# Adjacency product of a GNN layer, rearranged: x stationary, adj streamed 512 nodes wide into two alternating PSUM banks

## The chip, the core and the metric

The program runs on one core of a Trainium2 chip. The metric is the device time of one execution in microseconds; the kernel before takes 399.12 us (median of 3 runs, 398.97 to 399.54). "PE" is TensorE, "DVE" VectorE, "ACT" ScalarE, "POOL" GpSimd, "SP" SyncE, from whose queue the DMAs are issued.

## The reference

```python
support = x @ weight                                 # x (4096, 256), weight (256, 256)
h = (1.0 - t) * support + t * (adj @ support)        # adj (4096, 4096), about 0.1% full, t a scalar (1.0 in the data)
out = layernorm(x + h)                               # over the 256 features, eps 1e-5, all float32
```

Since the products are linear, h is also ((1 - t) x + t (adj @ x)) @ weight. The kernel before forms the product with weight first, the changed one last.

## The kernel before

Every float32 operand is split into a high part, rounded to the PE's float32r format (`*_hi`, a Copy on ACT), and a low part, the difference (`*_lo`, a subtraction on DVE or POOL). A product of two such operands is three products: high by high, high by low, low by high. In a matmul on the PE one operand, 128x128, is loaded first and stays (the stationary one, a LDWEIGHTS in the trace), and the other streams past it, one column per step.

**S stage** (`s_round`, L319): S = x @ W for 32 tiles of 128 nodes. Transposed x arrives in 16 chunks of 256 KB (`load_x`, L116, four slots); ACT makes `x_hi` (L168), POOL `x_lo` (L215). For a tile, six matmuls of 256 columns (L331, L336, L341) add up in half of a PSUM bank `s_ps`; a bank holds two tiles, so twelve matmuls in a row write one bank. ACT (L173) writes the high part of S beside the low part (DVE, L247), so that S has 512 columns per block of 128 nodes, high then low.

**Adjacency stage** (`adj_round`, L345): for each of 32 tiles of 128 output nodes, and each of 32 blocks j of 128 input nodes, the stationary operand is a 128x128 block of transposed adj. `high()` (L361) streams the 512 columns of S[j] past the high part of the block; `low()` (L366) streams the 256 high columns of S[j] past its low part, into the right half of the same bank. A tile owns one bank (`agg[u]`, u the parity of the tile), so 64 matmuls in a row write one bank. adj comes in 64 chunks of 1 MB (`load_adj`, L120), four slots (two per tile); ACT makes `a_hi` (L180), DVE `a_lo` (L253), each in one instruction of 2048 elements per partition.

```python
if j == 0:            # L368
    high()
    last = low()
else:
    low()
    last = high()
```

**Layer norm** (`layernorm`, L256), once per tile on DVE: two additions that take the halves of the bank with t and `base` (L260, L263), statistics (L266, L270), a square root on ACT (L184), reciprocal with one Newton step (L274 to L283), `normed` (L287), store by SP (L130). `base` = (1-t) S + x is POOL's (L220 to L231).

The order is written out by hand for each engine. PE goes through the S stage and then the tiles, and waits for `a_lo_ready` of a slot (L351) and for the reader of the bank it takes next (L348). ACT and DVE split the chunks of the next pair of tiles while PE works on this one; `a_high` waits for the loaded chunk and for PE's last use of the slot (`a_used`, L179). SP refills a slot as soon as DVE is done with its raw data (L146).

Of the kernel before, what the change touches and what calls it, by code (L numbers as in the profile page):

```python
# [6 lines left out]
P = 128  # L18
CHUNK_BLOCKS = 16
RING = 4  # L20
X_TILES = 2
X_RING = 4
# [3 lines left out]
def at_start(n):  # L26

    return isinstance(n, int) and n == 0


def gnn_layernorm_kernel(nc, xT, x, adjT, t, W, out):
# [3 lines left out]
    nodes, feats = x.shape  # L35
    TILES = nodes // P
    KT = feats // P
    CHUNK = CHUNK_BLOCKS * P
    PER_TILE = TILES // CHUNK_BLOCKS
    PAIRS = TILES // 2  # L40
    X_CHUNKS = TILES // X_TILES
    S_ROUNDS = X_CHUNKS // X_RING
    assert PER_TILE == 2 and RING == 2 * PER_TILE and S_ROUNDS <= RING

    ctx = ExitStack()
    with ctx:
# [9 lines left out]

# [3 lines left out]
        x_raw = sb("x_raw", [P, X_RING, KT, X_TILES * P])  # L60
        x_hi = sb("x_hi", [P, X_RING, KT, X_TILES * P], f32r)
        x_lo = sb("x_lo", [P, X_RING, KT, X_TILES * P], f32r)
        S = sb("S", [P, TILES, 2 * feats], f32r)
        a_raw = sb("a_raw", [P, RING, CHUNK])
        a_hi = sb("a_hi", [P, RING, CHUNK], f32r)
        a_lo = sb("a_lo", [P, RING, CHUNK], f32r)
        t_col = sb("t_col", [P, 1])
        omt_col = sb("omt_col", [P, 1])
        x_rows = sb("x_rows", [P, 2, feats])
        base = sb("base", [P, 2, feats])  # L70
        s_sum = sb("s_sum", [P, 2, feats])
# [11 lines left out]
        normed = sb("normed", [P, 2, feats])


        s_ps = [ctx.enter_context(nc.psum_tensor(f"s_ps{i}", [P, X_TILES, feats], f32)) for i in range(X_RING)]
        agg = [ctx.enter_context(nc.psum_tensor(f"agg{i}", [P, 2 * feats], f32)) for i in range(2)]


        w_loaded, t_loaded = sem("w_loaded"), sem("t_loaded")  # L90
# [24 lines left out]
        def _(sp):  # L115
# [16 lines left out]
            for slot in range(X_RING):  # L132
                load_x(slot, slot)
# [269 lines left out]
```

## Time and profile before

| | us |
|---|---|
| median of 3 runs | 399.12 |
| span of the profiled execution, first to last instruction | 397.6 |
| PE busy | 384.0 (97%) |
| DVE busy | 273.1 (69%) |
| ACT busy | 185.1 (47%) |
| POOL busy | 87.9 (22%) |

The profiled execution has no device time of its own beside its span; the median stands 1.5 us above the span. The span is counted from the first to the last instruction of the core. Matmuls are pipelined and the end of each is modelled, so busy time of PE says little of how long a matmul keeps it; the distance between the starts of two neighbouring matmuls says it.

### The profile page before, as it was taken

How to read it: one execution, taken by the hardware profiler on the slowest of the kernel's cores; microseconds unless marked ns; L12 is line 12 of the kernel's file. 1: busy time of each engine (PE TensorE's matmuls, PEld its weight loads, DVE VectorE, ACT ScalarE, POOL GpSimd, SP SyncE). 2: the span in 40 equal slices, each digit the busy share in tenths (PEclk: the TensorE clock that was granted, in tenths of full speed). 3: DMA queues.
4: the chain of work that ended last, by engine and by line, in shares of the span. 5: the costliest groups of instructions: out<-in, count | busy, mean ns of one | idle time of the engine just before them, and what ended most of it. 6: DMA issues, size and time to landing. Idle time of an engine off the chain costs nothing.

```text
span 397.6 us, 6141 instructions
## 1 busy us (share of the span) xinstructions
PE 384.0 (97%) x2240; PEld 336.6 (85%) x2240; DVE 273.1 (69%) x402; ACT 185.1 (47%) x160; POOL 87.9 (22%) x68
## 2 busy tenths in 40 slices
PE   4989999999999999999999999999999999999994
PEld 3978888888888888888888888888888888888883
DVE  1438977777676767777676767777676767777622
ACT  5669535445452635445353635445353635445200
POOL 5765923030300203030200303030200303030100
PEclk9999999999999999999999999999999999999998
DMA  6996966675554665676554665675554664670000
GB/s 185 309 305 222 343 233 235 219 250 211 209 205 170 240 223 176 208 257 211 203 205 176 238 220 176 213 257 211 201 207 176 232 226 172 218 257 13 0 26 13
DMA packets 20900, 80.02 MB, mean 201 GB/s; under 512 B 2208, under 2 KB 10656, under 8 KB 12704
## 3 DMA queue, kind: packets, MB, share of 16 engines
q1 hardware_dynamic: 20624, 79.70, 57.0%
q10 hardware_dynamic: 272, 0.26, 0.2%
q8 instruction: 3, 0.05, 0.0%
q14 instruction: 1, 0.01, 0.0%
HBM read 75.76 MB, written 4.19 MB: 201 GB/s over the span
## 4 chain that ended last, share of the span: by engine, by line
PE 91%; DMA 4%; ACT 2%; DVE 2%; POOL 1%; issue 1%; ACTq 0%; DVEq 0%
PE agg L361 60%; PE agg L366 30%; DMA x_raw<-in_xT 4%; ACT x_hi L168 1%; POOL x_lo L215 1%; DVE a_lo L253 1%; ACT a_hi L180 0%; DVE w_lo L291 0%; PE s_ps L336 0%; ACT S L173 0%; PE s_ps L341 0%; ACT w_hi L189 0%; DVE y_part L260 0%; DVE y L263 0%; DVE stats L266 0%
## 5 line engine op out<-in xcount | busy, mean ns | idle before, releaser
L361 PE MATMUL agg<-S,a_hi 128*128 128x512 f32 x1024 | 356.4, 396 | 0.4 <-DVE a_lo L253 0.4
L366 PE MATMUL agg<-S,a_lo 128*128 128x256 f32 x1024 | 280.3, 279 | 0.0
L361 PEld LDWEIGHTS agg<-S,a_hi 128*128 128x128 f32 x1024 | 189.9, 188 | 44.0 <-DVE a_lo L253 0.6
L253 DVE TENSOR_TENSOR a_lo<-a_raw,a_hi 128x2048 fp32r<-128x2048 f32 x64 | 150.6, 2358 | 70.3 <-ACT a_hi L180 70.3
L366 PEld LDWEIGHTS agg<-S,a_lo 128*128 128x128 f32 x1024 | 192.9, 188 | 2.8
L180 ACT ACTIVATE a_hi<-a_raw 128x2048 fp32r<-128x2048 f32 x64 | 122.2, 1913 | 67.8 <-PE agg L361 67.7
L231 POOL TENSOR_TENSOR base<-s_scaled,x_rows 128x512 f32<-128x512 f32 x16 | 22.6, 1411 | 272.2 <-DVE y L263 272.1
L184 ACT ACTIVATE std<-var_eps 128x1 f32<-128x1 f32 x32 | 6.5, 203 | 126.1 <-DVE var_eps L272 126.1
L287 DVE TENSOR_SCALAR normed<-y,mean_var,rstd 128x256 f32<-128x256 f32 x32 | 24.5, 765 | 2.5
L220 POOL TENSOR_TENSOR s_sum<-S 128x512 f32 (+1 forms) x16 | 24.5, 1531 | 4.7 <-DVE S L247 4.7
L260 DVE SCALAR_TENSOR_TENSOR y_part<-agg,t_col,base 128x256 f32<-128x256 f32 x32 | 15.3, 478 | 11.2 <-PE agg L361 11.2
L215 POOL TENSOR_TENSOR x_lo<-x_raw,x_hi 128x512 fp32r<-128x512 f32 x16 | 20.7, 1314 | 10.0 <-ACT x_hi L168 9.5
L223 POOL TENSOR_TENSOR s_scaled<-s_sum,omt_col 128x512 f32<-128x512 f32 x16 | 20.5, 1282 | 1.3
L247 DVE TENSOR_TENSOR S<-s_ps,S 128x512 f32 (+1 forms) x16 | 10.8, 688 | 14.1 <-ACT S L173 14.1
L180 ACT ACT_TABLE_LOAD x15 | 19.2, 1283 | 2.5 <-issue 2.5
L331 PE MATMUL s_ps<-w_hi,x_hi 128*128 128x256 f32 x64 | 13.7, 297 | 6.5 <-ACT w_hi L189 5.5
L184 ACT ACT_TABLE_LOAD x15 | 19.2, 1283 | 0.3
L263 DVE SCALAR_TENSOR_TENSOR y<-agg,t_col,y_part 128x256 f32<-128x256 f32 x32 | 15.5, 484 | 1.1
L331 PEld LDWEIGHTS s_ps<-w_hi,x_hi 128*128 128x128 f32 x64 | 10.6, 204 | 6.7 <-ACT x_hi L168 6.7
L283 DVE TENSOR_TENSOR rstd<-newton_c,rstd 128x1 f32<-128x1 f32 x32 | 14.3, 447 | 1.1
L266 DVE BATCH_NORM_STATS2 stats<-y 128x6 f32<-128x256 f32 x32 | 13.7, 428 | 1.1
L341 PE MATMUL s_ps<-w_hi,x_lo 128*128 128x256 f32 x64 | 13.4, 293 | 0.6 <-POOL x_lo L215 0.6
(18 smaller groups left out, 87.1 us busy)
## 6 DMA issues: line engine op xcount, KB each, us to landing
a_raw<-in_adjT SPq DMA_DIRECT2D x64, 1024.0 KB, 4.8
x_raw<-in_xT SPq DMA_DIRECT2D x16, 256.0 KB, 4.3
x_rows<-in_x SPq DMA_DIRECT2D x16, 256.0 KB, 3.3
out<-normed SPq DMA_DIRECT2D x32, 128.0 KB, 1.7
w_raw<-in_W ACTq DMA_DIRECT2D x1, 256.0 KB, 4.0
t_col<-in_t SPq DMA_DIRECT2D x1, 0.5 KB, 4.2
```

The costliest lines, as they stand in the source:

```text
L180: nc.scalar.activation(a_hi[:, slot], a_raw[:, slot], ACT.Copy).then_inc(a_hi_ready[slot], 1)
L184: nc.scalar.activation(std[:, :], var_eps[:, :], ACT.Sqrt).then_inc(std_ready, 1)
L215: nc.gpsimd.tensor_tensor(x_lo[:, slot], x_raw[:, slot], x_hi[:, slot].bitcast(f32), ALU.subtract).then_inc(x_lo_ready[slot], 1)
L220: nc.gpsimd.tensor_tensor(s_sum[:, :, :], s_pair[:, :, 0:feats], s_pair[:, :, feats:2 * feats], ALU.add).then_inc(s_sum_ready, 1)
L223: nc.gpsimd.tensor_tensor(s_scaled[:, :, :], s_sum[:, :, :], omt_col[:, :].unsqueeze(2).broadcast_to([P, 2, feats]), ALU.mult).then_inc(s_ ...
L231: nc.gpsimd.tensor_tensor(base[:, :, :], s_scaled[:, :, :], x_rows[:, :, :], ALU.add).then_inc(base_ready, 1)
L253: nc.vector.tensor_tensor(a_lo[:, slot], a_raw[:, slot], a_hi[:, slot].bitcast(f32), ALU.subtract).then_inc(a_lo_ready[slot], 1)
L263: nc.vector.scalar_tensor_tensor(y[:, :], agg[u][:, feats:2 * feats], t_col[:, :], y_part[:, :], ALU.mult, ALU.add).then_inc(y_ready[u], 1)
L287: nc.vector.tensor_scalar(normed[:, u], y[:, :], mean_var[:, 0:1], rstd[:, :], ALU.subtract, ALU.mult).then_inc(normed_ready, 1)
L331: nc.tensor.matmul(s_ps[slot][:, h], x_hi[:, slot, k, cols], w_hi[:, k], start=(k == 0), stop=False)
L361: return nc.tensor.matmul(agg[u][:, :], a_hi[:, slot, cols], S[:, j], start=(j == 0), stop=(j == TILES - 1))
L366: return nc.tensor.matmul(agg[u][:, feats:], a_lo[:, slot, cols], S[:, j, 0:feats], start=False, stop=False)
```

## The change

`S` and the S stage are gone. x itself, 128 nodes by 128 features at a time, is the stationary operand (`x_hi`, `x_lo`, kept whole in SBUF), and transposed adj streams past it 512 output nodes wide. The output nodes come in 8 chunks (`CHUNKS`) of 512; the 32 blocks of input nodes in 8 groups (`GROUPS`) of 4. The result is transposed, features by nodes, in two banks per chunk: `agg[c % 2][0]` for features 0 to 127 and `agg[c % 2][1]` for 128 to 255. For each block six matmuls of 512 columns are issued (`alternate`), in which one bank and the other take turns; only in the last group of a chunk `products` finishes one bank and then the other, twelve matmuls in a row each. `make_z` forms z = t (adj @ x) + (1 - t) x, transposed (the second term from `xt`, loaded and scaled by POOL); ACT and DVE split z, and `project` multiplies by W with z stationary, 24 matmuls of 256 columns per chunk, into four other banks. PE does that for chunk c-1 behind the first group of chunk c. The layer norm runs once per chunk over four tiles. The slots of adj hold 1 MB as before, now 4 blocks by 512 nodes. At the start PE runs 9 matmuls on zeros, the first group of adj is loaded and split in four pieces, and a table for the square root is loaded once ahead; all loops are unrolled. In the diff, the removed lines are those of the kernel above and mostly left out.

```diff
 import concourse.bass as bass
+WIDE = 512
+GROUP = 4
-X_TILES = 2
-X_RING = 4
+X_RING = 3
+WARM = 9
...
-        S = sb("S", [P, TILES, 2 * feats], f32r)
+        x_raw = sb("x_raw", [P, X_RING, GROUP, feats])
+        x_hi = sb("x_hi", [P, BLOCKS, feats], f32r)
+        x_lo = sb("x_lo", [P, BLOCKS, feats], f32r)
+        a_raw = sb("a_raw", [P, RING, GROUP, WIDE])
+        a_hi = sb("a_hi", [P, RING, GROUP, WIDE], f32r)
+        a_lo = sb("a_lo", [P, RING, GROUP, WIDE], f32r)
+        xt = sb("xt", [P, 2, KT, WIDE])
+        rows = sb("rows", [P, 2, TILES, feats])
+        z = sb("z", [P, KT, WIDE])
+        z_hi = sb("z_hi", [P, KT, WIDE], f32r)
+        z_lo = sb("z_lo", [P, KT, WIDE], f32r)
...
+        def y_tile(i):
+            return x_raw[:, 0, i]
+
+        def normed(c):
+            return x_raw[:, 1 + c % 2]
+
+        agg = [[ctx.enter_context(nc.psum_tensor(f"agg{i}{k}", [P, WIDE], f32)) for k in range(KT)]
+               for i in range(2)]
+        out_ps = [ctx.enter_context(nc.psum_tensor(f"out_ps{i}", [P, WIDE], f32)) for i in range(TILES)]
...
+        def turn(c, g):
+            return 2 * c + g // RING
...
+            def load_adj(c, g):
+                slot = g % RING
+                if turn(c, g):
+                    sp.wait_ge(a_lo_ready[slot], turn(c, g))
+                sp.dma_start(a_raw[:, slot], adjT[c * GROUPS + g]).then_inc(a_loaded[slot], 16)
+
+            def load_xt(c):
+                if c >= 2:
+                    for k in range(KT):
+                        sp.wait_ge(z_ready[k], c - 1)
+                sp.dma_start(xt[:, c % 2], xT[c]).then_inc(xt_loaded[c % 2], 16)
+
+            def load_rows(c):
+                if c >= 2:
+                    for i in range(TILES):
+                        sp.wait_ge(y_ready[i], c - 1)
+                sp.dma_start(rows[:, c % 2], x_sta[:, c * TILES:(c + 1) * TILES]).then_inc(rows_loaded[c % 2], 16)
...
+            load_x(0)
+            for b in range(GROUP):
+                landed = a0_loaded[b] if b < GROUP - 1 else a_loaded[0]
+                sp.dma_start(a_raw[:, 0, b], adjT[0, :, b]).then_inc(landed, 16)
...
+            for g in range(1, GROUPS):
+                load_x(g)
+                load_adj(0, g)
+            load_adj(1, 0)
+            load_xt(0)
...
+            for c in range(1, CHUNKS):
+                for g in range(1, GROUPS):
+                    load_adj(c, g)
+                    if g == 2:
+                        load_xt(c)
+                    if g == 5:
+                        load_rows(c)
+                if c + 1 < CHUNKS:
+                    load_adj(c + 1, 0)
+                store(c - 1)
...
+            def z_high(c):
+                for k in range(KT):
+                    act.wait_ge(z_ready[k], c + 1)
+                    if c:
+                        act.wait_ge(prod_ready[TILES - 1], c)
+                    nc.scalar.activation(z_hi[:, k], z[:, k], ACT.Copy).then_inc(z_hi_ready[k], 1)
...
+            act.preload_act_table_set("sqrt_and_others")
+            x_high(0)
+            for b in range(GROUP):
+                act.wait_ge(a0_loaded[b] if b < GROUP - 1 else a_loaded[0], 16)
+                nc.scalar.activation(a_hi[:, 0, b], a_raw[:, 0, b], ACT.Copy
+                                     ).then_inc(a0_hi_ready if b < GROUP - 1 else a_hi_ready[0], 1)
...
+            for g in range(1, GROUPS):
+                x_high(g)
+                a_high(0, g)
...
+            for c in range(1, CHUNKS):
+                for g in range(GROUPS):
+                    if g == RING - 1:
+                        z_high(c - 1)
+                    a_high(c, g)
+                    if g == RING:
+                        root(c - 1)
+            z_high(CHUNKS - 1)
+            root(CHUNKS - 1)
...
+            def scale_xt(c):
+                pool.wait_ge(xt_loaded[c % 2], 16 * (c // 2 + 1))
+                nc.gpsimd.tensor_tensor(xt[:, c % 2], xt[:, c % 2],
+                                        omt_col[:, :].unsqueeze(2).broadcast_to([P, KT, WIDE]), ALU.mult
+                                        ).then_inc(xt_scaled, 1)
+
+            nc.gpsimd.memset(z_hi[:, 0].bitcast(f32), 0.0).then_inc(zeros_ready, 1)
+            for g in range(GROUPS):
+                x_low(g)
...
+            def make_z(c):
+                dve.wait_ge(xt_scaled, c + 1)
+                for k in range(KT):
+                    if k == 0:
+                        dve.wait_ge(agg0_ready, c + 1)
+                    else:
+                        dve.wait_ge(a_used[RING - 1], turn(c, GROUPS - 1) + 1)
+                    if c:
+                        dve.wait_ge(z_hi_ready[k], c)
+                        dve.wait_ge(z_lo_ready[k], c)
+                    nc.vector.scalar_tensor_tensor(z[:, k], agg[c % 2][k][:, :], t_col[:, :], xt[:, c % 2, k],
+                                                   ALU.mult, ALU.add).then_inc(z_ready[k], 1)
+                for k in range(KT):
+                    dve.wait_ge(z_hi_ready[k], c + 1)
+                    if c:
+                        dve.wait_ge(prod_ready[TILES - 1], c)
+                    nc.vector.tensor_tensor(z_lo[:, k], z[:, k], z_hi[:, k].bitcast(f32), ALU.subtract
+                                            ).then_inc(z_lo_ready[k], 1)
...
+            def layernorm(c):
+                dve.wait_ge(rows_loaded[c % 2], 16 * (c // 2 + 1))
+                for i in range(TILES):
+                    dve.wait_ge(prod_ready[i], c + 1)
+                    if c:
+                        dve.wait_ge(normed_ready, c * TILES)
+                    nc.vector.tensor_tensor(y_tile(i), out_ps[i][:, 0:feats], rows[:, c % 2, i], ALU.add
+                                            ).then_inc(y_ready[i], 1)
+                    dve.wait_ge(y_ready[i], c + 1)
+                    nc.vector.bn_stats(stats[:, i], y_tile(i)).then_inc(stats_ready, 1)
+                for i in range(TILES):
+                    dve.wait_ge(stats_ready, c * TILES + i + 1)
+                    nc.vector.bn_aggr(mean_var[:, i], stats[:, i]).then_inc(mean_var_ready, 1)
...
+                for i in range(TILES):
+                    nc.vector.tensor_scalar(normed(c)[:, i], y_tile(i), mean_var[:, i, 0:1], rstd[:, i:i + 1],
+                                            ALU.subtract, ALU.mult).then_inc(normed_ready, 1)
...
+            for c in range(1, CHUNKS):
+                for g in range(GROUPS):
+                    if g == RING - 1:
+                        make_z(c - 1)
+                    a_low(c, g)
+                    if g == RING:
+                        layernorm(c - 1)
+            make_z(CHUNKS - 1)
+            layernorm(CHUNKS - 1)
...
+            def products(c, slot, j, b, k, first, last):
+                bank = agg[c % 2][k][:, :]
+                cols = slice(k * P, (k + 1) * P)
+                nc.tensor.matmul(bank, x_hi[:, j, cols], a_hi[:, slot, b], start=first, stop=False)
+                nc.tensor.matmul(bank, x_hi[:, j, cols], a_lo[:, slot, b], start=False, stop=False)
+                return nc.tensor.matmul(bank, x_lo[:, j, cols], a_hi[:, slot, b], start=False, stop=last)
+
+            def alternate(c, slot, j, b):
+                for k in range(KT):
+                    nc.tensor.matmul(agg[c % 2][k][:, :], x_hi[:, j, k * P:(k + 1) * P], a_hi[:, slot, b],
+                                     start=(j == 0), stop=False)
+                for k in range(KT):
+                    nc.tensor.matmul(agg[c % 2][k][:, :], x_hi[:, j, k * P:(k + 1) * P], a_lo[:, slot, b],
+                                     start=False, stop=False)
+                for k in range(KT):
+                    last = nc.tensor.matmul(agg[c % 2][k][:, :], x_lo[:, j, k * P:(k + 1) * P], a_hi[:, slot, b],
+                                            start=False, stop=False)
+                return last
+
+            def group(c, g):
+                slot = g % RING
+                pe.wait_ge(a_lo_ready[slot], turn(c, g) + 1)
+                if c == 0:
+                    pe.wait_ge(x_lo_ready, g + 1)
+                if c >= 2 and g == 0:
+                    for k in range(KT):
+                        pe.wait_ge(z_ready[k], c - 1)
+                if g < GROUPS - 1:
+                    for b in range(GROUP):
+                        done = alternate(c, slot, g * GROUP + b, b)
+                else:
+                    for k in range(KT):
+                        for b in range(GROUP):
+                            j = g * GROUP + b
+                            done = products(c, slot, j, b, k, False, j == BLOCKS - 1)
+                        if k == 0:
+                            done.then_inc(agg0_ready, 1)
+                done.then_inc(a_used[slot], 1)
+
+            def project(c):
+                for k in range(KT):
+                    pe.wait_ge(z_lo_ready[k], c + 1)
+                for i in range(TILES):
+                    if c:
+                        pe.wait_ge(y_ready[i], c)
+                    cols = slice(i * P, (i + 1) * P)
+                    dst = out_ps[i][:, 0:feats]
+                    for k in range(KT):
+                        nc.tensor.matmul(dst, z_hi[:, k, cols], w_hi[:, k], start=(k == 0), stop=False)
+                        nc.tensor.matmul(dst, z_hi[:, k, cols], w_lo[:, k], start=False, stop=False)
+                        done = nc.tensor.matmul(dst, z_lo[:, k, cols], w_hi[:, k], start=False, stop=(k == KT - 1))
+                    done.then_inc(prod_ready[i], 1)
+
+            pe.wait_ge(zeros_ready, 1)
+            for _ in range(WARM):
+                nc.tensor.matmul(out_ps[0][:, :], z_hi[:, 0, 0:P], z_hi[:, 0], start=True, stop=True)
+            first_group()
+            for g in range(1, GROUPS):
+                group(0, g)
+            pe.wait_ge(w_lo_ready, 1)
+            for c in range(1, CHUNKS):
+                group(c, 0)
+                project(c - 1)
+                for g in range(1, GROUPS):
+                    group(c, g)
+            project(CHUNKS - 1)
...
+    x_sta = x.reshape(blocks, P, feats).transpose(1, 0, 2)
+    xT = x.reshape(chunks, WIDE, feats // P, P).transpose(0, 3, 2, 1)
+    adjT = adj.reshape(chunks, WIDE, blocks // GROUP, GROUP, P).transpose(0, 2, 4, 3, 1)
+    adjT = adjT.reshape(chunks * (blocks // GROUP), P, GROUP, WIDE)
```

## Rows read from the trace of the kernel before

**Rows 1.** The page: span, busy time, slices, DMA rate, chain by engine.
```profile
span 397.6 us, 6141 instructions
PE 384.0 (97%) x2240; PEld 336.6 (85%) x2240; DVE 273.1 (69%) x402; ACT 185.1 (47%) x160; POOL 87.9 (22%) x68
...
PEclk9999999999999999999999999999999999999998
DMA  6996966675554665676554665675554664670000
GB/s 185 309 305 222 343 233 235 219 250 211 209 205 170 240 223 176 208 257 211 203 205 176 238 220 176 213 257 211 201 207 176 232 226 172 218 257 13 0 26 13
...
PE 91%; DMA 4%; ACT 2%; DVE 2%; POOL 1%; issue 1%; ACTq 0%; DVEq 0%
```

**Rows 2.** Groups of instructions by line: busy us, mean ns, idle before.
```profile
L361 PE MATMUL agg<-S,a_hi 128*128 128x512 f32 x1024 | 356.4, 396 | 0.4 <-DVE a_lo L253 0.4
L366 PE MATMUL agg<-S,a_lo 128*128 128x256 f32 x1024 | 280.3, 279 | 0.0
L253 DVE TENSOR_TENSOR a_lo<-a_raw,a_hi 128x2048 fp32r<-128x2048 f32 x64 | 150.6, 2358 | 70.3 <-ACT a_hi L180 70.3
L180 ACT ACTIVATE a_hi<-a_raw 128x2048 fp32r<-128x2048 f32 x64 | 122.2, 1913 | 67.8 <-PE agg L361 67.7
L215 POOL TENSOR_TENSOR x_lo<-x_raw,x_hi 128x512 fp32r<-128x512 f32 x16 | 20.7, 1314 | 10.0 <-ACT x_hi L168 9.5
L168 ACT ACTIVATE x_hi<-x_raw 128x512 fp32r<-128x512 f32 x16 | 10.0, 628 | 7.0 <-DMA x_raw<-in_xT 7.0
L247 DVE TENSOR_TENSOR S<-s_ps,S 128x512 f32 x12 | 8.3, 692 | 14.1 <-ACT S L173 14.1
```

**Rows 3.** Busy time and granted clock by stretch: start, first tile, 30 tiles, last.
```profile
core 0: us, PE busy (x) PEld busy (x) DVE busy (x) ACT busy (x) POOL busy (x), PEclk, DMA share, GB/s
0.00:33.36 33.36, 25.47 (x193) 24.59 (x193) 12.16 (x16) 21.01 (x35) 20.94 (x20) 1.00 0.81 267
33.36:44.69 11.33, 11.33 (x64) 9.88 (x65) 11.33 (x8) 8.86 (x6) 8.66 (x3) 1.00 0.72 259
44.69:380.59 335.90, 335.90 (x1921) 292.52 (x1921) 243.82 (x360) 154.79 (x118) 58.28 (x46) 1.00 0.57 202
380.59:391.68 11.09, 11.09 (x65) 9.61 (x64) 2.89 (x10) 0.20 (x1) 0.00 (x0) 1.00 0.03 12
391.68:397.60 5.92, 0.24 (x1) 0.00 (x0) 2.89 (x10) 0.20 (x1) 0.00 (x0) 0.77 0.07 22
```

**Rows 4.** Chain of waits, one row per tile boundary: start us, us, what.
```profile
44.69 0.47 PE agg L361 x2
55.78 0.46 PE agg L361 x2
67.08 0.47 PE agg L361 x2
...
380.59 0.47 PE agg L361 x2
391.68 0.25 PE agg L361
```

**Rows 5.** Timeline of PE, first matmuls of the S stage: start us, us, instruction.
```profile
7.25 0.63 PE L341 MATMUL s_ps<-w_hi,x_lo 128*128 128x256 f32 x2
7.68 0.63 PE L331 MATMUL s_ps<-w_hi,x_hi 128*128 128x256 f32 x2
8.10 0.63 PE L336 MATMUL s_ps<-w_lo,x_hi 128*128 128x256 f32 x2
8.53 0.63 PE L341 MATMUL s_ps<-w_hi,x_lo 128*128 128x256 f32 x2
8.96 0.52 PE L331 MATMUL s_ps<-w_hi,x_hi 128*128 128x256 f32 x2
```

**Rows 6.** The same timeline, middle of the S stage; the matmuls at 14.83 open a new bank.
```profile
14.59 0.40 PE L341 MATMUL s_ps<-w_hi,x_lo 128*128 128x256 f32 x2
14.71 0.31 PEld L331 LDWEIGHTS s_ps<-w_hi,x_hi 128*128 128x128 f32 x2
14.83 0.40 PE L331 MATMUL s_ps<-w_hi,x_hi 128*128 128x256 f32 x2
14.95 0.31 PEld L336 LDWEIGHTS s_ps<-w_lo,x_hi 128*128 128x128 f32 x2
15.07 0.40 PE L336 MATMUL s_ps<-w_lo,x_hi 128*128 128x256 f32 x2
...
24.67 0.40 PE L341 MATMUL s_ps<-w_hi,x_lo 128*128 128x256 f32 x2
```

**Rows 7.** Timeline of PE around the tile boundary at 44.7 us.
```profile
44.17 0.40 PE L361 MATMUL agg<-S,a_hi 128*128 128x512 f32 x1
44.41 0.28 PE L366 MATMUL agg<-S,a_lo 128*128 128x256 f32 x1
44.52 0.63 PE L361 MATMUL agg<-S,a_hi 128*128 128x512 f32 x2
44.99 0.39 PE L366 MATMUL agg<-S,a_lo 128*128 128x256 f32 x2
```

**Rows 8.** Chain of waits, the start: start us, us, what.
```profile
0.75 3.31 DMA x_raw<-in_xT
4.08 0.63 ACT x_hi L168
...
11.82 5.30 DMA x_raw<-in_xT
```

**Rows 9.** Timeline of all engines behind the last matmul.
```profile
391.95 0.48 DVE L260 SCALAR_TENSOR_TENSOR y_part<-agg,t_col,base 128x256 f32<-128x256 f32 x1 [7.59 <-PE agg L361]
...
392.99 0.43 DVE L266 BATCH_NORM_STATS2 stats<-y 128x6 f32<-128x256 f32 x1
395.05 0.41 DVE L287 TENSOR_SCALAR normed<-y,mean_var,rstd 128x256 f32<-128x256 f32 x1
```

More of the change, by code:

```diff
@@ L83, in gnn_layernorm_kernel @@
[L83 to L90, printed above, removed]
-        w_hi_ready, w_lo_ready = sem("w_hi_ready"), sem("w_lo_ready")
-        omt_ready = sem("omt_ready")
+        stats = sb("stats", [P, TILES, 6])
+        mean_var = sb("mean_var", [P, TILES, 2])
@@ L182, in root, with x_high, a_high @@
-            def root(tile):
-                act.wait_ge(var_eps_ready, tile + 1)
+            def x_high(g):
+                act.wait_ge(x_loaded[g % X_RING], 16 * (g // X_RING + 1))
+                nc.scalar.activation(x_hi[:, g * GROUP:(g + 1) * GROUP], x_raw[:, g % X_RING], ACT.Copy
+                                     ).then_inc(x_hi_ready, 1)
+            def a_high(c, g):
+                slot = g % RING
+                act.wait_ge(a_loaded[slot], 16 * (turn(c, g) + 1))
+                if turn(c, g):
+                    act.wait_ge(a_used[slot], turn(c, g))
+                nc.scalar.activation(a_hi[:, slot], a_raw[:, slot], ACT.Copy).then_inc(a_hi_ready[slot], 1)
@@ L188, in _ @@
-            act.wait_ge(w_loaded, 16)
-            nc.scalar.activation(w_hi[:, :, :], w_raw[:, :, :], ACT.Copy).then_inc(w_hi_ready, 1)
-            for slot in range(1, X_RING):
-                x_high(0, slot)
-            with act.Fori(0, S_ROUNDS - 1) as rnd:
-                for slot in range(X_RING):
-                    s_high(rnd, slot)
-                    x_high(rnd + 1, slot)
-            a_high(0, 0)
-            for slot in range(X_RING):
-                s_high(S_ROUNDS - 1, slot)
@@ L199, in _ @@
-            for slot in range(1, RING):
-                a_high(0, slot)
-            with act.Fori(0, PAIRS - 1) as pair:
-                for u in range(2):
-                    a_high(pair + 1, 2 * u)
-                    a_high(pair + 1, 2 * u + 1)
-                    root(pair * 2 + u)
-            root(TILES - 2)
-            root(TILES - 1)
+            act.preload_act_table_set("sqrt_and_others")
[4 more added lines that the diff above has]
+                                     ).then_inc(a0_hi_ready if b < GROUP - 1 else a_hi_ready[0], 1)
@@ L234, in _, with x_low @@
-            pool.wait_ge(omt_ready, 1)
-            for slot in range(X_RING):
-                pool.wait_ge(s_lo_ready[slot], S_ROUNDS)
-            make_base(0)
-            with pool.Fori(1, PAIRS) as pair:
-                make_base(pair)
+            def x_low(g):
+                pool.wait_ge(x_hi_ready, g + 1)
+                nc.gpsimd.tensor_tensor(x_lo[:, g * GROUP:(g + 1) * GROUP], x_raw[:, g % X_RING],
+                                        x_hi[:, g * GROUP:(g + 1) * GROUP].bitcast(f32), ALU.subtract
+                                        ).then_inc(x_lo_ready, 1)
@@ L242, in _ @@
+            for c in range(CHUNKS):
+                scale_xt(c)
         @block.vector
         def _(dve):
[L244 to L249 removed]
```

321 lines of the change are left out of this document (93 added, 228 removed).

## The prediction

> **What bounds the kernel now.** The page comes first: PE is busy for 97% of the span and holds 91% of the chain that ended last, while DVE, ACT and POOL have 69%, 47% and 22% [rows 1]. Then the groups: in 2048 matmuls PE was idle 0.4 us for an operand, whereas DVE waited 70.3 us for ACT, and ACT 67.7 us for PE to release slots [rows 2]. So the side engines follow PE. Then the stretches: 33.36 us before the first adjacency matmul, 358.3 us of adjacency stage (11.33 + 335.90 + 11.09) without idle time of PE, 5.92 us behind the last matmul's start [rows 3]. DMA is 57% busy in the middle, so it doesn't bound either. What counts is how long PE needs per matmul, and what lies before and behind the stage.
>
> **How long a matmul keeps PE.** Durations in the rows overlap; distances of starts are read. The thirty tiles between 44.69 and 380.59 take 11.197 us each [rows 4], 349.9 ns for a pair of 512 and 256 columns. In the middle of the S stage starts of 256-column matmuls lie 0.24 us per two apart, from 14.59 to 24.67 in 42 such steps, so 120 ns each [rows 6]. Earlier the distance is 0.425 us per two, 213 ns each [rows 5], and at 8.96 it falls. 256 columns in 213 ns is 1.2 a nanosecond: until about 9 us PE ran at the lower level, 1.2 GHz, after having waited up to 5.5 us (the granted clock printed for that stretch, 1.00, doesn't show it). At 2.4 GHz the streaming takes half of that, 106.7 ns for 256 columns and 213.3 for 512. So a 256-column matmul costs 13.3 ns over its streaming, and a pair costs 349.9 - 320.0 = 29.9, or 15.0 per matmul. Both kinds of row agree on a fixed cost per matmul of 13 to 15 ns, whatever the width, that the lower clock hides.
>
> **The change, part by part.**
>
> *Columns of the main product.* Before: 1024 x (512 + 256) = 786,432. After: 8 chunks x 32 blocks x 6 x 512 = 786,432. Nothing is saved in streaming; the number of matmuls falls from 2048 to 1536.
>
> *Cost of one such matmul.* No row shows 512 columns behind 512 columns in alternating banks. Bounds: below, pure streaming, 213.3 ns. Above, 232.5: at a tile boundary two 512-column matmuls follow each other in different banks, and the two last 0.63 us where one lasts 0.40 [rows 7], so their starts are some 0.23 apart; in the chain the two take 0.46 or 0.47 at every boundary, 232.5 ns each [rows 4]. I take 213.3 + 13.3 = 226.7, since the S stage is the nearest stream of equal widths and repeats to 10 ns in 10 us; the boundary is a single place in which the order of high and low also turns round.
>
> *The alternation itself.* I cost it at nothing. In the S stage a bank ends after twelve matmuls; the step into the new one at 14.83 is 0.24 us per two like all others [rows 6], and the boundary of rows 7 changes bank too and gains nothing. What speaks for a gain is only that a single change is not the same as a change at each matmul.
>
> The Trainium skill, "TensorE: Matmul & The Clock Gate", section "Wait — 56ns, not 53.3ns?", has a fixed cost of about 2.5 ns for back-to-back matmuls at the full clock. The trace does not agree: its rows show five times that. By the skill's figure a 512-column matmul would come to 215.8 ns, an estimate, and the sum below to 378, close to rival A.
>
> *S stage removed, project added.* Both are 192 matmuls of 256 columns. At 120 ns a project costs 24 x 0.12 = 2.9 us; seven lie between groups, 20.2 us. Does PE wait for z? The second half of z needs the last group; behind it come a DVE operation of 512 columns from PSUM (0.7, as S L247), a Copy (0.63) and a subtraction (0.65): about 2.1 us with semaphores [rows 2]. Group 0 of the next chunk covers that with 24 x 0.2267 = 5.4 us. Without cover it would be 7 x 2.1 = 15 us. In DVE's queue make_z stands ahead of the fourth `a_low`, which PE needs more than 10 us later.
>
> *Layer norm.* Per chunk four tiles, 9 to 10 us of DVE, with eight `a_low` at 2.36 (18.9) and z (2.7) some 31 us of the 46 that PE needs. ACT's `a_high` for group 5 stands behind the square root, hence behind half a layer norm; from there to PE's need of that group are some 8 us. I cost it at nothing. The table loads of 1.28 us each go, but ACT is not the bound: nothing.
>
> *Start.* PE's stage began at 33.36. Now it needs x group 0 and adj group 0. The first 256 KB landed at 4.06 [rows 8]; 512 KB are put at 5, `x_hi` of 1024 columns 1.1 and `x_lo` on POOL 2 x 1.31 [rows 2], so PE starts near 8.7. The 9 matmuls on zeros end before, at about 4.5, so part of group 0 may run at 1.2 GHz (24 matmuls in up to 9 us). It doesn't decide: group 1 is complete only with 3.4 MB. The fullest slices moved 305 to 343 GB/s with the DMA engines 90% busy [rows 1]; at 330 and with 2 us to the first byte that is 12.6 us, then `a_hi` 1.9 and `a_lo` 2.4: group 1 starts at 17.0. From there each group brings 1.57 MB in 4.8 us, less than PE's 5.4: chunk 0 is PE-bound, narrowly. Bounds 14.5 (sooner data, which group 0 then limits) and 20 (300 GB/s).
>
> *End.* Behind the last matmul: z 2.1; project, of which the first tile is ready after 0.9; then four times an addition and statistics (0.95 each by [rows 9]) until 4.7 after project's start; aggregation to rstd 1.62 as before, between 393.43 and 395.05, plus 0.7 for three more tiles and one more operation; `normed` 4 x 0.41; store and end 2.1 as before [rows 9]. Together 2.1 + 4.7 + 2.3 + 1.6 + 2.1 + 0.1 for the drain = 12.9, against 5.9 now. Bounds 11 and 15.
>
> *Sum.* 17.0 + 1512 x 0.2267 (342.8, without group 0) + 20.2 + 0.2 (last matmul's own drain) + 12.9 = 393.1 us of span, against 397.6: start and project cost 33.4 before and 11.6 + 20.2 after, the end 7 more, the main product 10 less. The median stands 1.5 us over the span of before; so 394.6. About 0.2% (0.8 us) is what a measurement can tell from no change.
>
> **Rivals.**
>
> *A: the fixed cost mostly goes*, because same-bank or unequal neighbours caused it. Each matmul then takes 213.3 (none left) to 218 (a third left), say 215.5: 17.0 + 325.8 + 33.3 + 1.5 = 377.6. For: pairs in tiles of one parity take 11.30 us, of the other 11.09 [rows 4], with the same instructions, so order and place matter by some ns; rows 5 show none of the cost. Against: no bank change in rows 6 or 7 was cheaper. Chance 0.33. A half gain (220 ns) gives 384.5: 0.10.
>
> *B: slower.* In the adjacency stage a 512-column matmul already keeps PE 232.5 ns and the 256-column one the rest of 349.9, 117; then 512-wide streams gain nothing in the stage (1512 x 0.2325 = 351.5, with group 0's share 357), and the longer end and the project decide: 403.4. The place is each 512-column matmul in a stream, and it turns slower from 229.7 ns on. For: the starts in rows 7, 44.17 to 44.41 and 44.52 to 44.99. Against: the S stage's 13.3, which would then depend on width. Chance 0.19.
>
> *C: the clock.* The granted clock is 1.00 through the stage, PE being busy without gap [rows 3]. If taking turns between banks opened small gaps and the clock dropped to 1.2 GHz for a tenth of the stage, 512 columns would take twice their 213 ns there [rows 5] and the sum rise by some 30 us, to 425. Chance 0.02. The Trainium skill, same page, section "A second HAM failure mode: psum-queue depth-cycling", reports such an oscillation for a kernel that cycles through banks.
>
> *D: no difference*, 229 to 230 ns or a start and end later by 4 us together: 399. Chance 0.04.
>
> **Numbers.** The forecast, 394.6, has 0.32 (its own range, 390 to 399, from the bounds of start and end). Faster: 0.31 of it, A 0.33, the half gain 0.10, together 0.74; same 0.05 (D and the forecast's edge); slower 0.21. The range runs from 376 (A with an early start) to 405 (B with a late end) and leaves out C and the tails.
>
> **What would show it.** Starts of `agg` matmuls 0.227 apart (A 0.216, B 0.232), equal in the alternating groups and in each chunk's last group, which stays in one bank; if the last group's are wider, alternation pays and I am wrong on it. First full group near 17 us; PE idle under 0.1 us ahead of each project; steps of 120 ns in it; 12 to 14 us behind the last `agg` matmul. Idle time of PE before `agg` for a_lo in chunk 1 or later would make wrong what I costed at nothing.

## The result, and the profile after

The changed kernel takes 396.92 us (median of 6 runs, 395.71 to 397.23), the kernel before 399.31 (6 runs): ratio 0.9935, 95% interval 0.9916 to 0.9955, faster by 0.65%. Forecast were 394.6 and 1.1% under the median then shown (399.12). The profiled execution took 396.9 with a span of 395.1, so 1.8 us lie outside the span. The forecast gain was 4.5 us, the measured one 2.4. One execution of the kernel with one bank in every group, below, showed a granted clock of 0.749 and took 485.83 us, where its others had 0.986 to 0.994, and is left out of its figures.

Lines of the page after (busy us, share; slices; chain by engine; groups as in [rows 2]):

```profile
span 395.1 us, 4192 instructions
PE 380.6 (96%) x1737; PEld 317.3 (80%) x1737; DVE 228.1 (58%) x277; ACT 144.0 (36%) x101; POOL 44.0 (11%) x21
...
GB/s 245 422 421 387 323 401 211 220 235 168 237 215 173 254 261 173 203 239 228 223 177 214 235 187 256 214 159 267 219 171 212 235 225 229 199 53 2 0 1 53
...
PE 90%; DVE 4%; DMA 3%; SPq 1%; issue 1%; ACT 1%; DVEq 0%
...
L236 DVE TENSOR_TENSOR a_lo<-a_raw,a_hi 128x2048 fp32r<-128x2048 f32 x63 | 155.6, 2478 | 128.4 <-ACT a_hi L174 128.4
L330 PE MATMUL agg<-a_hi,x_hi 128*128 128x512 f32 x448 | 139.6, 393 | 4.1 <-DVE a_lo L297 3.6
```

PE still bounds: it waited 4.1 us for operands at this line, nearly all ahead of group 0, while DVE and ACT wait longer than before. L330, L333 and L336 are `alternate`, L324 to L326 `products`, L381 to L383 `project`. The stretches (columns as in [rows 3]), cut at the start of group 1, the end of chunk 0's last matmul and the end of the last `agg` matmul (ends as modelled, some 0.17 us behind the streams):

```profile
8.70:17.42 8.72, 8.59 (x24) 6.48 (x24) 4.21 (x4) 6.14 (x7) 3.20 (x2) 0.65 1.02 422
17.42:56.55 39.13, 38.66 (x169) 31.70 (x170) 34.67 (x12) 22.00 (x15) 26.32 (x8) 1.00 0.98 383
56.55:381.50 324.95, 324.95 (x1513) 272.07 (x1511) 180.45 (x235) 111.35 (x75) 11.37 (x6) 1.00 0.54 195
381.50:395.10 13.60, 4.50 (x25) 4.32 (x24) 8.00 (x25) 0.83 (x2) 0.00 (x0) 0.70 0.12 39
```

Timeline of PE in the middle: first the last group of a chunk, twelve matmuls into one bank, then the end of a project and an alternating stretch:

```profile
100.11 0.39 PE L324 MATMUL agg<-a_hi,x_hi 128*128 128x512 f32 x1
...
100.79 0.39 PE L324 MATMUL agg<-a_hi,x_hi 128*128 128x512 f32 x1
...
111.02 0.28 PE L383 MATMUL out_ps<-w_hi,z_lo 128*128 128x256 f32 x1
111.14 0.63 PE L330 MATMUL agg<-a_hi,x_hi 128*128 128x512 f32 x2
...
112.53 0.61 PE L330 MATMUL agg<-a_hi,x_hi 128*128 128x512 f32 x2
112.98 0.62 PE L333 MATMUL agg<-a_lo,x_hi 128*128 128x512 f32 x2
113.43 0.62 PE L336 MATMUL agg<-a_hi,x_lo 128*128 128x512 f32 x2
113.89 0.39 PE L330 MATMUL agg<-a_hi,x_hi 128*128 128x512 f32 x1
```

Alternating: six starts in 113.89 - 112.53 = 1.36 us, 226.7 ns each. In one bank: from 100.11 to 100.79 three, 226.7 each. The first six behind the 256-column matmuls of the project, from 111.14 to 112.53, take 1.39 us, 232 each; this adds some 28 ns per chunk. The chain shows the period of a chunk, counted at group 1: 192 x 226.7 + 24 x 120 and these 20 to 30 ns make 46.42 us.

```profile
64.88 0.47 PE agg L330 x2
...
111.30 0.47 PE agg L330 x2
...
343.40 0.47 PE agg L330 x2
```

| term, us | forecast | measured |
|---|---|---|
| until group 1 starts | 17.0 | 17.4 |
| 1512 matmuls of 512 columns | 342.8 (226.7 ns) | 342.7 (226.7 ns) |
| seven projects | 20.2 | 20.3 (46.42 - 43.52 each) |
| waits and wider starts of PE in chunk 0 | 0 | 0.9 |
| behind the last `agg` matmul's stream | 13.1 | 13.8 |
| outside the span | 1.5 | 1.8 |
| sum | 394.6 | 396.9 |

Of the 0.9 us, 0.6 is a wait at group 3: its first start comes at 29.08 where the stream before it was through at 28.46. The rest is wider starts at the beginning of groups 1 and 3 (0.56 and 0.47 us per two, in place of 0.453). The wait in the chain:

```profile
5.42 11.47 DMA a_raw<-in_adjT
16.91 1.93 ACT a_hi L174
18.86 2.92 DVE a_lo L236
21.79 2.81 DVE w_lo L303
24.66 4.37 DVE a_lo L236
29.08 0.73 PE agg L330 x2
```

`w_lo`, 512 elements per partition, took 2.8 us and the `a_lo` behind it 4.4 where it takes 2.3 alone: POOL's `x_lo` ran beside both. The end, in the timeline:

```profile
383.79 0.55 PE L381 MATMUL out_ps<-w_hi,z_hi 128*128 128x256 f32 x1 [2.28 <-DVE z_lo L255]
384.14 0.42 PE L382 MATMUL out_ps<-w_lo,z_hi 128*128 128x256 f32 x1
384.36 0.42 PE L383 MATMUL out_ps<-w_hi,z_lo 128*128 128x256 f32 x1
...
387.05 0.28 PE L381 MATMUL out_ps<-w_hi,z_hi 128*128 128x256 f32 x1
387.17 0.28 PE L382 MATMUL out_ps<-w_lo,z_hi 128*128 128x256 f32 x1
```

Having idled 2.3 us for z, PE runs the first 14 of the last project's 24 matmuls at the lower level, 1.2 GHz (starts 213 ns apart until 386.9), the others 120 ns apart.

### The profile page after: what moved, and what is told of

Same layout as the page of the kernel before. It is cut to its first block, busy times and chain, and to the rows that moved or that the text cites. A ratio compares the mean times of both kernels' runs of the same rounds, so it can differ in the third digit from the quotient of the medians.

```text
span 395.1 us, 4192 instructions
## 1 busy us (share of the span) xinstructions
PE 380.6 (96%) x1737; PEld 317.3 (80%) x1737; DVE 228.1 (58%) x277; ACT 144.0 (36%) x101; POOL 44.0 (11%) x21
## 4 chain that ended last, share of the span: by engine, by line
PE 90%; DVE 4%; DMA 3%; SPq 1%; issue 1%; ACT 1%; DVEq 0%
PE agg L330 24%; PE agg L333 24%; PE agg L336 24%; PE agg L326 4%; PE agg L324 4%; PE agg L325 4%; DMA a_raw<-in_adjT 3%; PE out_ps L381 2%; PE out_ps L382 2%; PE out_ps L383 2%; DVE a_lo L236 2%; DVE w_lo L303 1%; ACT a_hi L174 0%; SPq L136 0%; SPq L107 0%
## 5 line engine op out<-in xcount | busy, mean ns | idle before, releaser
L330 PE MATMUL agg<-a_hi,x_hi 128*128 128x512 f32 x448 | 139.6, 393 | 4.1 <-DVE a_lo L297 3.6
L333 PE MATMUL agg<-a_lo,x_hi 128*128 128x512 f32 x448 | 138.9, 391 | 0.0
L336 PE MATMUL agg<-a_hi,x_lo 128*128 128x512 f32 x448 | 138.9, 391 | 0.0
L330 PEld LDWEIGHTS agg<-a_hi,x_hi 128*128 128x128 f32 x448 | 84.2, 190 | 22.3 <-issue 4.0
L333 PEld LDWEIGHTS agg<-a_lo,x_hi 128*128 128x128 f32 x448 | 84.8, 189 | 17.9
L336 PEld LDWEIGHTS agg<-a_hi,x_lo 128*128 128x128 f32 x448 | 84.7, 189 | 17.9
L214 POOL TENSOR_TENSOR x_lo<-x_raw,x_hi 128x1024 fp32r<-128x1024 f32 x8 | 27.4, 3438 | 11.5 <-ACT x_hi L166 11.3
L324 PE MATMUL agg<-a_hi,x_hi 128*128 128x512 f32 x64 | 24.9, 389 | 0.0
L325 PE MATMUL agg<-a_lo,x_hi 128*128 128x512 f32 x64 | 24.9, 389 | 0.0
L326 PE MATMUL agg<-a_hi,x_lo 128*128 128x512 f32 x64 | 24.9, 389 | 0.0
L381 PE MATMUL out_ps<-w_hi,z_hi 128*128 128x256 f32 x64 | 18.9, 295 | 2.3 <-DVE z_lo L255 2.3
L382 PE MATMUL out_ps<-w_lo,z_hi 128*128 128x256 f32 x64 | 18.7, 293 | 0.0
L383 PE MATMUL out_ps<-w_hi,z_lo 128*128 128x256 f32 x64 | 18.6, 291 | 0.0
L381 PEld LDWEIGHTS out_ps<-w_hi,z_hi 128*128 128x128 f32 x64 | 12.9, 202 | 2.9 <-DVE z_lo L255 2.7
```

What stands on the lines that cost most here:

```text
L214: nc.gpsimd.tensor_tensor(x_lo[:, g * GROUP:(g + 1) * GROUP], x_raw[:, g % X_RING], x_hi[:, g * GROUP:(g + 1) * GROUP].bitcast(f32), ALU.s ...
L324: nc.tensor.matmul(bank, x_hi[:, j, cols], a_hi[:, slot, b], start=first, stop=False)
L325: nc.tensor.matmul(bank, x_hi[:, j, cols], a_lo[:, slot, b], start=False, stop=False)
L326: return nc.tensor.matmul(bank, x_lo[:, j, cols], a_hi[:, slot, b], start=False, stop=last)
L330: nc.tensor.matmul(agg[c % 2][k][:, :], x_hi[:, j, k * P:(k + 1) * P], a_hi[:, slot, b], start=(j == 0), stop=False)
L333: nc.tensor.matmul(agg[c % 2][k][:, :], x_hi[:, j, k * P:(k + 1) * P], a_lo[:, slot, b], start=False, stop=False)
```

## The experiments

The theory: a matmul on float32r operands keeps PE for its columns at 2.4 GHz plus some 13.3 ns, whichever bank it writes, so the change gains by 512 matmuls fewer. The rivals: bank, width, unequal neighbours. Ratios are to the kernel before, timed beside each. Spans of single executions are named where a part of the time is read from a trace.

### One bank in every group

```diff
-                    for b in range(GROUP):
-                        done = alternate(c, slot, g * GROUP + b, b)
+                    for k in range(KT):
+                        for b in range(GROUP):
+                            done = products(c, slot, g * GROUP + b, b, k, g * GROUP + b == 0, False)
```

> The changed kernel with products() in every group: 12 matmuls in a row write one bank, as in its own last groups, where starts already lie 226.7 ns apart. Theory (a fixed cost of 13.3 ns per matmul, whatever the bank): agg starts 226.7 ns apart everywhere, time 396.9 within 0.8 us. Rival (taking turns between banks is what keeps it at 226.7 in the seven other groups): wider there by 5 ns or more, 1300 x 5 ns = 6.5 us slower or more.

396.51 us (median of four), ratio 0.9933 (0.9911 to 0.9955), against 0.9935 with alternation. The timeline of its middle:

```profile
100.36 0.39 PE L324 MATMUL agg<-a_hi,x_hi 128*128 128x512 f32 x1
...
101.04 0.39 PE L324 MATMUL agg<-a_hi,x_hi 128*128 128x512 f32 x1
```

226.7 ns again: taking turns between banks does nothing here.

### Two matmuls of 256 columns for one of 512

```diff
-                for k in range(KT):
-                    nc.tensor.matmul(agg[c % 2][k][:, :], ..., a_hi[:, slot, b], ...)
+                for h in range(2):
+                    half = slice(h * 256, (h + 1) * 256)
+                    for k in range(KT):
+                        nc.tensor.matmul(agg[c % 2][k][:, half], ..., a_hi[:, slot, b, half], ...)
...
```

> The changed kernel with every matmul of 512 columns in the alternating groups (1344 of 1536) issued as two of 256 columns; the same columns in all. Theory (fixed cost per matmul): 2688 matmuls at 120 ns in place of 1344 at 226.7, so 322.6 in place of 304.7 us, 17.9 us slower, 414.8. Rival (the cost grows with the columns, 6% of them): no change, 397. A third way, PE bound by its instructions: more than 120 ns each.

412.88 us, ratio 1.0351 (1.0329 to 1.0372): 16 us slower than the changed kernel, with starts 120 ns apart (0.24 for two):

```profile
100.01 0.40 PE L335 MATMUL agg<-a_lo,x_hi 128*128 128x256 f32 x2
100.25 0.40 PE L338 MATMUL agg<-a_hi,x_lo 128*128 128x256 f32 x2
```

Each matmul costs 13.3 ns over its stream at 256 and at 512 columns. That is the count's share in the time, shown by moving the count alone. The sum gave 17.9 us; the missing 1.9 are found in the trace: this kernel had no wait at group 3 (0.6), and its last project ran at the upper level from its start (1.2).

### Operands of 2 bytes, after and before

```diff
-    f32, f32r = mybir.dt.float32, mybir.dt.float32r
+    f32, f32r = mybir.dt.float32, mybir.dt.bfloat16
```

(with the `.bitcast(f32)` of the parts dropped), first in the changed kernel, later in the kernel before. The products keep fewer bits.

> The changed kernel with the high and low parts of all operands in bfloat16 in place of float32r (so the products keep fewer bits); the same matmuls, columns and banks. Theory (the 13.3 ns come from operands of 4 bytes, most likely from loading the stationary one): starts 213.3 to 216 ns apart, 1512 x 11 ns = 17 us faster, about 380. Rival (the cost belongs to every matmul with a new stationary operand, whatever its type): 226.7 ns, time 397 less what a faster DVE gives at the start, 1 us.

> The kernel before with the high and low parts of all operands in bfloat16 in place of float32r (the products keep fewer bits); everything else as before. Theory (what the change wins in the main product is only the fixed cost of 512 matmuls fewer and the pattern of unequal neighbours, both of which belong to 4-byte operands): a pair takes 320 + 2 x 2.6 = 325 ns in all tiles, 25 us less than 349.9, the S stage 192 x 11 ns = 2 less, 399.0 - 27 = 372; that is 6 us faster than the changed kernel in bfloat16 (378.0), so there the change would make it slower. Rival (unequal widths or one bank per tile cost time of their own): a pair stays 10 ns or more above 325, 382 or more.

After: 378.02 us, ratio 0.9481 (0.9463 to 0.9498). Before: 373.48 us, ratio 0.9354 (0.9326 to 0.9382). Their timelines, the changed kernel first:

```profile
100.01 0.59 PE L333 MATMUL agg<-a_lo,x_hi 128*128 128x512 bf16 x2
100.44 0.59 PE L336 MATMUL agg<-a_hi,x_lo 128*128 128x512 bf16 x2
100.87 0.59 PE L330 MATMUL agg<-a_hi,x_hi 128*128 128x512 bf16 x2
```

```profile
100.16 0.38 PE L361 MATMUL agg<-S,a_hi 128*128 128x512 bf16 x1
100.38 0.27 PE L366 MATMUL agg<-S,a_lo 128*128 128x256 bf16 x1
100.49 0.38 PE L361 MATMUL agg<-S,a_hi 128*128 128x512 bf16 x1
```

512 columns take 216 ns, 256 take 109 (325 for the pair): the fixed cost falls from 13.3 to 2.5 ns. The Trainium skill, "TensorE: Matmul & The Clock Gate", section "Wait — 56ns, not 53.3ns?", gives about 2.5 ns; these two runs agree, the float32r runs, with 13.3, don't. A pair takes 325 ns in every tile, without parity, so unequal neighbours and one bank per tile cost nothing of their own at 2 bytes. And the sign of the change turns: 0.9481 / 0.9354 = 1.014 (1.009 to 1.018 from the ends of the two intervals), the changed kernel is 1.4% the slower one.

### Where the cost sits: half of the stationary operand

```diff
+                m = P if j == 0 else P // 2
-                    nc.tensor.matmul(agg[c % 2][k][:, :], x_hi[:, j, k * P:(k + 1) * P], ...)
+                    nc.tensor.matmul(agg[c % 2][k][0:m, :], x_hi[:, j, k * P:k * P + m], ...)
...
```

> The changed kernel with only 64 of the 128 columns of the stationary operand in the alternating groups (but for block 0 of a chunk): half of the features of adj @ x is left out there; the streamed columns are the same 512. Theory (the 13.3 ns are the loading of a 4-byte stationary operand beside the stream, so they go with its columns): 213.3 + 6.7 = 220 ns between starts, 1296 x 6.7 ns = 8.6 us shorter, 388. Rival (a fixed cost of each matmul on 4-byte operands, or one of the streamed side): 226.7, 397.

One run, 400.99 us. Both expectations fail, as its timeline and its loads of the stationary operand show:

```profile
90.06 0.62 PE L331 MATMUL agg<-a_hi,x_hi 128*64 128x512 f32 x2
...
91.44 0.62 PE L331 MATMUL agg<-a_hi,x_hi 128*64 128x512 f32 x2
...
92.81 0.62 PE L331 MATMUL agg<-a_hi,x_hi 128*64 128x512 f32 x2
```

```profile
L337 PEld LDWEIGHTS agg<-a_hi,x_lo 128*64 128x64 f32 x432 | 58.2, 135 | 41.4 <-issue 0.4
```

Six starts take 1.375 us here, 229 ns each: with half the columns to load, and loads of 135 ns in place of 189, the cost is 16 ns, not 6.7. So in these runs it comes with 4-byte operands and did not shrink with the stationary columns; what it is stays open. A stationary operand of 2 bytes beside a streamed one of 4 was not run. In bfloat16 a load of 128 columns took 98 ns, so the length of the load is not ruled out for good.

### The order of high and low in the kernel before

```diff
...
-                            if j == 0:
-                                high()
-                                last = low()
-                            else:
-                                low()
-                                last = high()
+                            high()
+                            last = low()
```

> The kernel before with high() ahead of low() in every block, not only for j = 0, so that the order never turns at a tile boundary. In the kernel before, tiles of one parity take 11.30 us and the others 11.10. Theory (the turn of the order at the boundary sets a slower pattern for every second tile): all tiles alike; if all at 11.10, 16 x 0.2 = 3.2 us faster, 396.1, if all at 11.30, 402.5. Rival (the bank or the slots of those tiles): parity stays, 399.3.

403.08 us, ratio 1.0096 (1.0067 to 1.0126). From its busy time by stretch, between the first matmuls of tile 1 and tile 30:

```profile
45.17:373.06 327.89, 327.89 (x1858) 284.35 (x1857) 238.66 (x349) 152.68 (x116) 57.03 (x45) 1.00 0.58 207
```

327.89 / 29 = 11.31 us for a tile, and every one takes 11.30 or 11.31. A pair then costs 353.3 ns, 33.3 over its streaming; in the kernel before that held for one parity, and 346.7 (26.7 over, twice 13.3) for the other. The turns of the order at the beginning of a tile (512 columns behind 512 at the boundary, 256 behind 256 one block later) are what sets the better pattern for every second tile; the edit takes out both. Why the patterns differ is open.

### The start and the end

Edits of the changed kernel:

```diff
# w_lo late
-                if g == 2:
+                if g == GROUPS - 1:
                     dve.wait_ge(w_hi_ready, 1)
# x_lo on DVE: x_low(g) moved from POOL to DVE, ahead of each group's a_low
# longer warm-up
-WARM = 9
+WARM = 20
# warm end, ahead of the last project
+TAIL = 9
...
+            for k in range(KT):
+                pe.wait_ge(z_ready[k], CHUNKS - 1)
+            for _ in range(TAIL):
+                nc.tensor.matmul(agg[CHUNKS % 2][0][:, :], x_hi[:, 0, 0:P], a_hi[:, 0, 0], start=True, stop=True)
# groups 1 and 2 in four pieces: on ACT, and in the same way on DVE and PE
+SPLIT = 3
...
+                if g < SPLIT:
+                    act.wait_ge(a_loaded[g], 16)
+                    for b in range(GROUP):
+                        nc.scalar.activation(a_hi[:, g, b], a_raw[:, g, b], ACT.Copy
+                                             ).then_inc(a0_hi_ready if b < GROUP - 1 else a_hi_ready[g], 1)
...
```

> The changed kernel with the splitting of W (w_lo, 2.9 us on DVE) and omt moved from behind the third group's a_lo to behind the last group's of chunk 0; nothing needs them before chunk 1. Theory (w_lo in DVE's queue makes a_lo of group 3 late, and PE waits 0.62 us at 29.1 us for it): that wait goes, chunk 0 ends 0.6 to 1 us sooner, 396.1. Rival (a_lo of group 3 is slow, 4.4 us, because POOL's x_lo runs beside it, and that alone makes it late): under 0.3 us.

395.14 us, ratio 0.9912 (0.9891 to 0.9933). In the trace the wait at group 3 is gone (it starts at 28.5, not 29.1) and the last group of chunk 0 starts 0.7 us sooner. The other 1.2 us of the span are the last project, which ran at 120 ns from its start, after the same idle 2.3 us:

```profile
383.10 0.36 PE L381 MATMUL out_ps<-w_hi,z_hi 128*128 128x256 f32 x1 [2.28 <-DVE z_lo L255]
383.30 0.28 PE L382 MATMUL out_ps<-w_lo,z_hi 128*128 128x256 f32 x1
```

Nothing in the edit touches that stage, so chance is the likelier reading. But the six spans of this kernel lie at 393.2 to 394.4, those of the changed kernel at 393.9 to 395.4, and the runs don't show that the edit has no part in it. Of the 1.8 us between the medians, 0.7 is accounted for by the edit.

> The changed kernel with x_lo made by DVE (ahead of each group's a_lo) in place of POOL. Theory (DVE and POOL slow each other in chunk 0: a_lo 2.29 us alone and up to 4.4 beside x_lo, x_lo 2.35 alone and up to 4.4 beside a_lo): a_lo 2.3 and x_lo about 1.2 us throughout, 3.5 per group, PE does not wait for group 3, chunk 0 ends 0.7 us sooner, 396.2. Rival (DVE's queue gets too long): a_lo of group 1 comes 1.2 us later than at 17.4 and the start moves by as much, 398.

394.84 us, ratio 0.9897 (0.9881 to 0.9912). Up to 40 us every whole `a_lo` takes 2.29 us and `x_lo` 1.2, as here at group 2:

```profile
18.68 2.29 DVE L228 TENSOR_TENSOR a_lo<-a_raw,a_hi 128x2048 fp32r<-128x2048 f32 x1 [0.34 <-ACT a_hi L174]
```

PE waits for nothing after group 1, whose start (17.3) did not move, and the last `agg` matmul comes 0.9 us sooner. So the two engines do hold each other up. The time is 1.4 us below what was expected; 1.2 of it are the last project, which ran at the upper level here too. The Trainium skill, "SBUF — State Buffer", section "Who interferes with whom", says that a DVE instruction with two SBUF inputs contends with a GpSimd one that reads SBUF; these traces agree (`a_lo` 2.29 us against up to 4.5, `x_lo` on POOL 2.35 against up to 4.5).

> The changed kernel with 20 matmuls on zeros at the start in place of 9, which reach to about 8 us, so that PE has no idle stretch before group 0. Theory (group 0 doesn't decide, since group 1 is not ready before 17.4): group 0's starts narrow from 427 to 227 ns, it ends near 14.2, PE waits longer for group 1, and the time stays within 0.5 us of 396.9. Rival (the slow clock in group 0 costs what it takes there, 13 x 0.2): 2.6 us faster. If the matmuls on zeros end after 8.7 us, up to 0.5 us slower.

397.23 us, ratio 0.9956 (0.9939 to 0.9974). Group 0 ran at full clock and ended near 14.8, PE waited for group 1, and the slow stretch came there:

```profile
14.33 0.62 PE L336 MATMUL agg<-a_hi,x_lo 128*128 128x512 f32 x2
17.71 1.22 PE L330 MATMUL agg<-a_hi,x_hi 128*128 128x512 f32 x2 [2.77 <-DVE a_lo L236]
18.73 1.05 PE L333 MATMUL agg<-a_lo,x_hi 128*128 128x512 f32 x2
```

Some 14 matmuls at 427 ns in group 1 put group 2 at 26.2, against 23.0. The time stayed inside what the theory gave, but by luck: chunk 0 ended 2.4 us later, and half of that came back because in this execution the last project ran at the upper level throughout. Here the longer warm-up gained nothing, because a wait followed it.

> The changed kernel with 9 more matmuls of 512 columns, into a bank that nothing reads, between the last agg matmul and the last project, while z is formed (2.3 us); they add no result. Theory (PE's clock falls in those 2.3 us and the first 13 or 14 matmuls of the last project run at 1.2 GHz, 213 in place of 120 ns): they run at 120, the layer norm's first tiles come 0.5 us and the last 1.2 us sooner, time 0.9 to 1.2 us less, 395.9. Rival (DVE's chain hides it): under 0.3 us.

396.08 us, ratio 0.9935 (0.9914 to 0.9957). The project runs at 120 ns and the span is 1.1 us shorter in the trace, as expected; the timed runs don't separate it from the changed kernel, whose own runs spread from 395.7 (mean granted clock 0.994) to 397.2 (0.985). Nor does the trace show that the extra matmuls did it. In seven float32r traces of kernels without them the last project began at the upper level five times (once it fell to the lower one after the first few matmuls, in the half-stationary kernel) and at the lower one twice, in the changed kernel and in the one with one bank. In the three with them it ran at the upper level throughout.

The next kernel has the late `w_lo`, the longer warm-up, the warm end and the four pieces; `x_lo` stays on POOL.

> The changed kernel with the edits of the three kernels before it, and the splitting of adj in groups 1 and 2 of chunk 0 in four pieces each, as group 0 has it, so that PE can start on a group with its first block. Theory (group 1 then starts near 14.5 instead of 17.4, as its adj lands at 13.1; group 0 warm ends at 14.2; later groups keep up): 2.9 for the start, 0.8 for the wait at group 3, 1.1 for the tail, 392.1. Rival (DMA in chunk 0, busy 98% there, holds back the later groups): the start's gain is given back in chunk 0, 394.8 to 395.8.

397.13 us, ratio 0.9948 (0.9927 to 0.9968), above the theory's 392.1 and above the rival's 395.8 too: the gain of the start was given back, though not by the data. Group 1 started at 14.9, then slow `a_lo` beside POOL's `x_lo` held PE at group 3 for 2.0 us. Behind it the clock fell once more (starts 427 ns apart from 30 to 33 us), and chunk 0 ended 1.0 us later than in the changed kernel:

```profile
17.67 6.30 DVE a_lo L314 x4
23.97 4.42 DVE a_lo L244
28.39 0.04 issue
28.44 0.74 PE agg L347 x2
```

The last one is that kernel with `x_lo` on DVE.

> The kernel e8_all with x_lo made by DVE. In e8_all PE started on group 1 at 14.9 but waited 2.4 us for the third piece of the queue, a_lo of group 3 (24 to 28.4 us), beside x_lo on POOL. adj of the groups lands 3.75 us apart, less than PE's 5.44. Theory (that wait is the slow a_lo, not the data): group 3 ready near 25.5, no wait after group 1, clock stays up, chunk 0 ends near 52.6 to 53.5 in place of 56.4, and with the warm end of 0.8: 396.9 - 3.3 - 0.8 = 392.8. Rival (data): PE waits at group 3 or 4 by 1.5 us or more, over 394.5.

392.39 us, ratio 0.9834 (0.9820 to 0.9848), the fastest version and 0.4 us from what was expected. PE starts group 1 at 14.6 and has no wait behind it until the end. Its chain:

```profile
14.56 0.70 PE agg L347 x2
61.21 0.47 PE agg L347 x2
```

## Why the prediction was right, and where it missed

The time lies 2.3 us above the forecast and inside its own range, and the mechanism is the forecast one. But the gain was only about half of the forecast 4.5 us, so small misses at both ends of the kernel weigh as much as what was gained.

*How long a matmul keeps PE* was right to 0.1 ns, and it decided the sum: 226.7, from the S stage's 120. *The alternation itself*, costed at nothing, was right; the whole-kernel run with one bank shows it.

*Rival A* (0.33) and the half gain (0.10) are false: no float32r matmul came below 226.7 ns, only bfloat16 gave 216. *Rival B* (0.19) is false: 512-column streams take 226.7. The start distance of 232.5 in rows 7 was read as the hold of one matmul in a stream. The trace after has the same 232 ns for the first six starts behind a project, and 226.7 from there on: such a distance stands behind a change of width and is not what a stream holds. The chance of A was too high for what rows 6 said. It leaned on the step between parities, which the runs put down to the order at the beginning of a tile, and on rows 5 showing none of the cost, which tells of the lower clock alone.

*C* and *D*: no drop of the clock from chunk 1 to the last `agg` matmul (granted clock 1.00, PE busy for 324.95 of 324.95 us); no difference was 2.4 us away.

*Start* came out at 17.4 for 17.0. The rate was right: from 2 us until group 1's adj landed at 13.1, DMA moved 333 GB/s on average (414 in the last 4.4 us of that). But 3.75 MB had moved by then, not 3.4: the loads of group 2, issued from 4.6 us on, were under way too. As written, the term also has a slip: 3.4 MB at 330 GB/s behind 2 us come to 12.3, not 12.6, and the slip hid part of the miss, by luck. "Group 0 doesn't decide" held: group 0, slow as it was, was through at 17.2, and at 14.8 with the longer warm-up, and group 1 started no sooner.

The 2.3 us by which the forecast was too low are four terms, the start being one of them (0.4). *Waits in chunk 0*, costed at nothing, were 0.9, of which 0.6 at group 3. The prediction priced `a_lo` at 2.4 us throughout and left out that the moved `w_lo` stands in DVE's queue ahead of group 3, and that DVE and POOL slow each other; taking away either of the two removed the wait. *End* was 0.7 over: the last project was priced at 120 ns, although PE idles for z just before, and in the profiled execution that cost 1.2 us; the other parts of the term came 0.5 lower than forecast (the end took 12.5 us where the project ran at 120 ns). *Outside the span*: 1.8 for 1.5.

Why the gain is small: the main product gave back 358.3 - 348.2 = 10 us, by 512 matmuls fewer (6.8) and by even neighbours in place of the worse pattern (16 tiles at 0.2, 3.2). The project, the longer start and the longer end together cost 7.6 more than the S stage and the old end (395.1 - 348.2 against 397.6 - 358.3).

## What to carry to other kernels

Take the price of a matmul from the steadiest stream of equal widths in the trace, as the distance of its starts less the streaming of its columns, and multiply by the count; with float32r 13 ns per matmul is worth cutting counts for, with bfloat16 it isn't, and the same rearrangement loses. Don't read the hold of one matmul from a single distance in a mixed pattern. Ahead of a bound engine's first work, list what else stands in the queues of its feeders and whether DVE and POOL run at once. A warm-up ahead of a wait of 2.8 us gained nothing here.

## What the runs showed of the hardware that was not expected

- The fixed cost per matmul over its streaming at 2.4 GHz: 13.3 ns with float32r operands, 2.5 with bfloat16, at 256 and 512 columns, in one bank or two; about 16 with a float32r stationary operand of 64 columns (one run).
- Pairs of 512 and 256 columns settle at 346.7 or 353.3 ns, by the order at the beginning of a tile.
- The printed granted clock can be 1.00 for stretches in which starts 427 ns apart show the lower level (the start of the kernel with `w_lo` late, 8.7 to 13.5 us). The distances are the better witness.
- After the same idle 2.3 us the clock is down in some executions and up in others (the last project, in seven traces: low from the start in two).
- A load stream of 1 MB and 512 KB pieces moved over 420 GB/s for some 20 us, against 343 in the fullest slice of the kernel before.
